# Norm roots as a power on GpSimd and softmax reciprocals between two 32x32 block transposes, in a transformer layer on one core

## The reference

```
x = x + layernorm(attention(layernorm(x)))
x = x + layernorm(ffn(layernorm(x)))

layernorm(x) = (x - mean) / sqrt(var + 1e-5)          # no weights
attention:  c_kv = x W_DKV + b, c_q = x W_DQ + b       # latent width 128
            k_c, v = c_kv W_UK + b, c_kv W_UV + b;  q_c = c_q W_UQ + b
            k_r, q_r = (x W_KR + b) * pe, (x W_QR + b) * pe
            per head (16 of width 32): k = [k_c, k_r], q = [q_c, q_r]
            softmax(q k^T / sqrt(32)) v, then W_O + b
ffn:        shared relu(x up)^2 down, plus 2 of 16 experts chosen per token
```

## Time and profile before

| | us |
|---|---|
| median of 3 runs | 1858.47 (1858.25 to 1858.62) |
| the profiled execution | 1858.86 |
| its span, first to last instruction | 1857.0 |
| attention units, all 32 | about 62 to 1085 of the span |

### The profile page before, as it was taken

The page is one execution under the profiler, slowest core; times in us unless marked ns, Lnnn a source line. Parts: engine busy times, 40 slices in busy tenths (PEclk is TensorE's granted clock), DMA queues, the critical chain, the costliest instruction groups (busy, mean ns, idle before and its releaser), DMA issues.

```text
span 1857.0 us, 21713 instructions
## 1 busy us (share of the span) xinstructions
PE 1703.8 (92%) x7194; PEld 1042.3 (56%) x7194; DVE 1030.8 (56%) x2133; ACT 828.4 (45%) x1465; POOL 726.6 (39%) x627
## 2 busy tenths in 40 slices
PE   5898989989989989989899788999999999988998
PEld 2444535435445445444444346888766666656886
DVE  2666577567676685684755635444511111116998
ACT  2345355355355454454454434443133333336554
POOL 0355465456455455563655642000122222214341
PEclk9798999989989999999989889999799999999999
DMA  5654455356355364462554332412473333448773
GB/s 157 174 155 123 121 143 181 84 152 181 86 165 152 93 187 123 136 190 77 150 162 150 100 114 79 164 46 97 132 264 131 126 127 132 127 141 299 240 240 123
DMA packets 123365, 270.51 MB, mean 146 GB/s; under 512 B 14996, under 2 KB 26644, under 8 KB 117108
## 3 DMA queue, kind: packets, MB, share of 16 engines
q1 hardware_dynamic: 96856, 205.93, 36.7%
q0 software_dynamic: 12912, 41.82, 7.1%
q10 hardware_dynamic: 13488, 21.37, 3.1%
HBM read 153.99 MB, written 92.01 MB: 132 GB/s over the span
## 4 chain that ended last, share of the span: by engine, by line
PE 66%; DVE 22%; DMA 4%; ACT 3%; issue 3%; POOL 1%; SPq 1%; DVEq 0%; ACTq 0%; POOLq 0%
PE bank L616 9%; PE bank L594 8%; PE bank L672 7%; PE bank L695 7%; DVE a L804 6%; PE bank L553 6%; PE bank L536 5%; PE bank L476 5%; DVE a L810 3%; PE bank L521 3%; PE bank L507 3%; PE bank L525 3%; PE bank L492 2%; PE bank L545 2%; DVE a L735 2%
## 5 line engine op out<-in xcount | busy, mean ns | idle before, releaser
L1449 POOL TENSOR_TENSOR a<-a 128x512 f32<-128x512 f32 x384 | 483.0, 1284 | 475.2 <-ACT a L1261 475.2
L1261 ACT ACTIVATE a<-bank 128x512 f32<-128x512 f32 x512 | 299.8, 595 | 258.2 <-PE bank L525 252.0
L804 DVE TENSOR_REDUCE a<-bank 128x1 f32<-128x512 f32 x512 | 325.2, 668 | 96.4 <-PE bank L507 95.9
L521 PE MATMUL bank<-a 128*128 128x512 f32 x512 | 281.6, 550 | 50.1 <-ACT a L1261 50.0
L507 PE MATMUL bank<-a 128*128 128x512 f32 x512 | 203.0, 434 | 28.5 <-DVE a L804 20.1
L525 PE MATMUL bank<-a 68*128 68x512 f32 x512 | 209.4, 409 | 0.3 <-ACT a L1251 0.2
L594 PE MATMUL bank<-c 128*128 128x512 f32 x768 | 186.8, 401 | 22.8 <-ACT c L1306 8.4
L521 PEld LDWEIGHTS bank<-a 128*128 128x128 f32 x512 | 100.1, 196 | 180.1 <-ACT a L1261 98.8
L1116 DVE TENSOR_TENSOR f<-f 128x256 f32<-128x256 f32 x79 | 33.6, 425 | 268.2 <-ACT f L1378 268.2
L594 PEld LDWEIGHTS bank<-c 128*128 128x128 f32 x768 | 146.2, 192 | 62.3 <-issue 13.2
L616 PE MATMUL bank<-c 128*128 128x512 f32 x768 | 176.8, 390 | 3.4 <-DVE c L854 1.7
(11 more groups left out here) (176 smaller groups left out, 2093.7 us busy)
## 6 DMA issues: line engine op xcount, KB each, us to landing
a<-kq_scratch SPq DMA_DIRECT2D x192, 256.0 KB, 5.6
kq_scratch<-a SPq DMA_DIRECT2D x32, 1024.0 KB, 4.1
a<-a SPq DMA_DIRECT2D x80, 256.0 KB, 5.0
yp_scratch<-f ACTq DMA_DIRECT2D x79, 256.0 KB, 2.0
a<-in_L_attn_x SPq DMA_DIRECT2D x15, 1024.0 KB, 8.5
x_scratch<-a SPq DMA_DIRECT2D x8, 1024.0 KB, 5.1
h_scratch<-a SPq DMA_DIRECT2D x8, 1024.0 KB, 4.3
hT_scratch<-a SPq DMA_DIRECT2D x8, 1024.0 KB, 6.5
```

Of the source, the lines that this page charges most:

```text
L521: e.matmul(SC[n % 2][:], K.Kc[:, z, j, i * P:(i + 1) * P], K.Qc[:, z, j, :], start=True, stop=False)
L804: e.tensor_reduce(K.mx[:, i, j:j + 1], K.MX[n % 3][:], AX.X, ALU.max).then_inc(Z.max, 1)
L1261: e.activation(K.pt[:, n % NP, :], K.SC[n % 2][:], ACT.Exp, scale=SCALE).then_inc(Z.exp, 1)
L1449: e.tensor_tensor(K.acc[:, j, :], a, K.pt[:, n % NP, :], ALU.add).then_inc(Z.acc, 1)
```

## The change

The change does four things.

- The norm's root leaves VectorE, with L742 and L759. GpSimd does it in eight instructions on 128x4 numbers: add epsilon, a power with exponent -0.5 (a tensor_tensor against a tile of -0.5), one Newton step in four, and offset and scale. Each but the last waits for the one before. It starts when the variances of the four tiles are there (semaphore var).
- A norm's labels are still seven: the three of the root are now pause, root, pause.
- ScalarE's copy of the denominators (L1274) is gone. VectorE reads them from PSUM with a block transpose (every 32x32 block for itself), takes the reciprocal of one column in 32, a 128x16 tile, and writes them back to 128x512 with a second block transpose that reads each number 32 times. The bank of "total" is given back by the reciprocal, so by VectorE's place in its order and no longer by ScalarE's.
- The labels of it are four in place of five: total, invert, pause, divide. GpSimd's multiplication is "divide", where it stood with the fourth reciprocal.

```diff
 def norm_order(kind, b):
-    return ([("stat", kind, b, 0), ("stat", kind, b, 1)] + [("root", kind, b, s) for s in range(3)]
-            + [("scale", kind, b, 0), ("scale", kind, b, 1)])
+    return [("stat", kind, b, 0), ("stat", kind, b, 1), ("pause",), ("root", kind, b), ("pause",), ("scale", kind, b, 0), ("scale", kind, b, 1)]
 def normalise_order(u):
-    return [("total", u)] + [("invert", u, n) for n in range(4)]
+    return [("total", u), ("invert", u), ("pause",), ("divide", u)]
 def vector_program
-    def invert(u, n):
-        cut = slice(n * P, (n + 1) * P)
+    def invert(u):
+        bank = begin("total", u)
+        if u:
+            w.wait_ge(Z.cx, u)
+        e.transpose(K.rden, bank[:]).then_inc(Z.dT, 1)
+        w.wait_ge(Z.dT, u + 1)
+        e.reciprocal(K.dr, K.rden[:, 0:S:HD]).then_inc(*end("total", u))
         m = K.fill["total", u]
         w.wait_ge(Z.free[m % 2], m // 2 + 1)
-        e.reciprocal(K.rden[:, cut], K.rden[:, cut]).then_inc(Z.rden, 1)
+        e.transpose(K.rden, K.dr.unsqueeze(2).broadcast_to([P, S // HD, HD])).then_inc(Z.rden, 1)
 def scalar_program
-    def total(u):
-        bank = begin("total", u)
-        if u:
-            w.wait_ge(Z.cx, u)
-        e.copy(K.rden, bank[:]).then_inc(*end("total", u))
 def gpsimd_program
-    def invert(u, n):
+    def divide(u):
         g = u % NG
-        if n == 3:
-            w.wait_ge(Z.kept, u + 1)
-            w.wait_ge(Z.rden, 4 * (u + 1))
-            e.tensor_tensor(K.ctxT[:, g, :], K.ctxT[:, g, :], K.rden, ALU.mult).then_inc(Z.cx, 1)
+        w.wait_ge(Z.kept, u + 1)
+        w.wait_ge(Z.rden, u + 1)
+        e.tensor_tensor(K.ctxT[:, g, :], K.ctxT[:, g, :], K.rden, ALU.mult).then_inc(Z.cx, 1)
+    def root(kind, b):
+        mv, nw = K.mv[kind], K.nw[kind]
+        ve, t, r = nw[:, 0, :], nw[:, 1, :], nw[:, 2, :]
+        w.wait_ge(Z.var[kind], 4 * (b + 1))
+        if b:
+            w.wait_ge(Z.scaled[kind], 4 * b)
+        e.tensor_scalar(ve, mv[:, :, 1], EPS, None, ALU.add).then_inc(*chain.next())
+        w.wait_ge(Z.root, chain.n)
+        w.wait_ge(Z.half, 1)
+        e.tensor_tensor(r, ve, K.mhalf, ALU.pow).then_inc(*chain.next())
+        w.wait_ge(Z.root, chain.n)
+        e.tensor_tensor(t, r, r, ALU.mult).then_inc(*chain.next())
...
+        e.tensor_tensor(r, r, t, ALU.mult).then_inc(*chain.next())
+        w.wait_ge(Z.root, chain.n)
+        e.tensor_tensor(nw[:, 3, :], mv[:, :, 0], r, ALU.mult).then_inc(Z.off[kind], 1)
+        e.tensor_scalar(nw[:, 4, :], r, -1.0, None, ALU.mult).then_inc(Z.off[kind], 1)
```

More of the change, by code:

```diff
@@ L288, in __init__ @@
         self.ones, self.small, self.sel, self.rope = make("ones_set"), make("dve_step"), make("sel_set"), make("rope_done")
+        self.var = {k: make(f"var_{k}") for k in KINDS}
         self.off = {k: make(f"off_{k}") for k in KINDS}
+        self.half, self.root = make("half_set"), make("root_step")
+        self.dT, self.dr = make("dT_done"), make("dr_done")
         self.scaled = {k: make(f"scaled_{k}") for k in KINDS}
@@ L342, in attention_room @@
     K.ones = tile([P, HD])
+    K.mhalf = tile([P, 4])
+    K.dr = tile([P, S // HD])
     K.stats = {"n": tile([P, 4, 6])}
@@ L721, in stat @@
     def stat(kind, b, half):
-        stats, mv, nw = K.stats[kind], K.mv[kind], K.nw[kind]
+        stats, mv = K.stats[kind], K.mv[kind]
         src = {"n": K.xt, "y": K.yb, "h": K.xb}[kind]
@@ L736, in stat @@
             at[i] = small.n
+        if b and not half:
+            w.wait_ge(Z.off[kind], 2 * b)
         for i in (2 * half, 2 * half + 1):
             w.wait_ge(Z.small, at[i])
[L739 to L759, removed]
+            e.bn_aggr(mv[:, i, :], stats[:, i, :]).then_inc(Z.var[kind], 1)
     def sel():
@@ L1173, in finish @@
         e.tensor_tensor(K.x1[:, z, :], K.x1[:, z, :], K.sh[:, z, :], ALU.add).then_inc(Z.co, 1)
-    stages = {"stat": stat, "root": root, "sel": sel, "proj": proj, "half": half, "bias": bias, "top": top, "invert": invert,
+    stages = {"stat": stat, "sel": sel, "proj": proj, "half": half, "bias": bias, "top": top, "invert": invert,
               "project": project, "route": route, "split h": split_h, "split up": split_up, "split down": split_down, "up": up,
@@ L1207, in scale @@
         src, out = {"n": (K.xt, K.xt), "y": (K.yb, K.yb), "h": (K.xb, K.yb)}[kind]
-        w.wait_ge(Z.off[kind], b + 1)
+        w.wait_ge(Z.off[kind], 2 * (b + 1))
         for i in (2 * half, 2 * half + 1):
@@ L1417, in scalar_program @@
     stages = {"scale": scale, "turn": turn, "proj": proj, "v": v, "half": half, "rows": rows, "scores": scores, "keep": keep,
-              "total": total, "turn2": turn2, "split h": split_h, "split up": split_up, "round up": round_up,
+              "turn2": turn2, "split h": split_h, "split up": split_up, "round up": round_up,
               "round down": round_down, "up": up, "store": store, "choose early": choose, "e turn": e_turn, "e up": e_up,
@@ L1436, in gpsimd_program @@
     e.memset(K.ones[:], 1.0).then_inc(Z.ones, 1)
+    e.memset(K.mhalf, -0.5).then_inc(Z.half, 1)
+    chain = Steps(Z.root)
     def scores(u, i, j):
@@ L1449, in scores @@
         e.tensor_tensor(K.acc[:, j, :], a, K.pt[:, n % NP, :], ALU.add).then_inc(Z.acc, 1)
-    def invert(u, n):
+    def divide(u):
         g = u % NG
-        if n == 3:
-            w.wait_ge(Z.kept, u + 1)
-            w.wait_ge(Z.rden, 4 * (u + 1))
-            e.tensor_tensor(K.ctxT[:, g, :], K.ctxT[:, g, :], K.rden, ALU.mult).then_inc(Z.cx, 1)
+        w.wait_ge(Z.kept, u + 1)
[14 more added lines that the diff above has]
+        w.wait_ge(Z.root, chain.n)
+        e.tensor_tensor(t, t, ve, ALU.mult).then_inc(*chain.next())
+        w.wait_ge(Z.root, chain.n)
+        e.tensor_scalar(t, t, 0.5, -1.5, ALU.mult, ALU.add).then_inc(*chain.next())
+        w.wait_ge(Z.root, chain.n)
+        e.tensor_tensor(r, r, t, ALU.mult).then_inc(*chain.next())
+        w.wait_ge(Z.root, chain.n)
+        e.tensor_tensor(nw[:, 3, :], mv[:, :, 0], r, ALU.mult).then_inc(Z.off[kind], 1)
+        e.tensor_scalar(nw[:, 4, :], r, -1.0, None, ALU.mult).then_inc(Z.off[kind], 1)
     def scale(kind, b, half):
@@ L1513, in gather @@
         e.indirect_dma_start(K.yc[:, z, :], None, K.yp_d, bass.IndirectOffsetOnAxis(K.sl2[:, t:t + 1], 0)).then_inc(Z.cg[z], 16)
-    stages = {"scores": scores, "invert": invert, "scale": scale, "split down": split_down, "choose early": choose,
+    stages = {"scores": scores, "divide": divide, "root": root, "scale": scale, "split down": split_down, "choose early": choose,
               "store": store, "fetch": fetch, "gather": gather}
@@ L1731, in program @@
     K.fill = {x: n for n, x in enumerate(x for x in K.order if x[0] in FILLS)}
-    K.at_root = {}
     with ExitStack() as ctx:
```

## The result

| | before | changed |
|---|---|---|
| median us, 5 runs each | 1858.25 (1857.02 to 1858.62) | 1875.33 (1868.7 to 1876.06) |
| ratio | 1 | 1.0085, 95% interval 1.0067 to 1.0102 |
| span of the profiled execution | 1857.0 | 1873.4 |
| TensorE's mean granted clock | 0.946 | 0.948 |

What follows compares the result with a forecast made beforehand. TensorE's waits were taken as the bound, chiefly 50.0 us for exponentials, plus lower clock behind them. Waits -33, clock -35, bank against maxima 0, last reciprocals -2 made -70 us from 1858.86: 1790, 8-in-10 range 1758 to 1862.

Steps and rivals of the forecast that it cites:

- bank against maxima: Before half q: TensorE's new wait for total's bank, about 50 us, offset by fewer waits for maxima; 0, ends -20 and +30.
- The clock: Behind the y and h scalings: shorter waits avoid the lower granted clock, 35 us back, 21 at h and 14 at y.
- The waits at the scalings: TensorE's waits for exponentials at seven y and seven h norms: 7.5 to 2.8 us a pair, 33 us saved.
- R: Length of a norm's root on GpSimd: 2.4 us taken, lower bound 1.6, upper 6.7.
- R - 1.4: TensorE's wait left at a norm h scaling: 1.0 us in place of 3.6.
- R - 0.6: TensorE's wait left at a norm y scaling: 1.8 us, where ScalarE stood 3.93 before.
- The last term: End of the kernel: the last unit's four reciprocals, which nothing hides, -2 us.
- GpSimd's queue behind the root: Three sums behind the root on GpSimd: late by half a microsecond, covered unless the root takes over about 4 us.
- rival (a): The root's power on GpSimd is slow, so scaling waits grow: about 1895 us; chance 0.18, three quarters of it slower.
- Rival (b): Before half q: slow transposes or unrecovered bank waits eat the gain, +30 to +45, 1820 to 1835 us; chance 0.14.
- Rival (c): In shorter units the stack through DRAM or GpSimd's load becomes a new bound: 1825 us; chance 0.13.
- the signs that it named for being wrong: Power over 2 us, clock still 0.55 behind waits of 1 to 2 us, or g = 0 units over 1 us longer.

Runs made afterwards that it cites:

- root_only: The kernel before with the norm part of the change alone (root on GpSimd, reciprocals as before): 1842.87 us, ratio 0.9928.
- recip_only: The kernel before with the reciprocal part of the change alone (two transposes and a 128x16 reciprocal, roots on VectorE): 1875.41 us, ratio 1.01.
- recip_early_only: The kernel before with the reciprocal part alone, VectorE's transposes and reciprocal issued at the label total: 1812.87 us, ratio 0.977.
- invert_early: The changed kernel with VectorE's two transposes and reciprocal issued at the label total, ahead of half k: 1806.32 us, ratio 0.9724.
- root_early: The changed kernel with the root two labels earlier, ahead of both pauses: 1855.7 us, ratio 0.9995.
- power_twice: The changed kernel with the power issued a second time in each root, same result: 1904.14 us, ratio 1.0255.

## Why the prediction was wrong, by its own steps

**The failing step is the pair "bank against maxima", put at 0.** Its first half was right nearly to the digit: 1.6 us a unit were forecast, 1.51 measured in three units of a batch, 2.12 in g = 0 where 2.2 was forecast, 48.3 us over 29 units against "about 50". The second half, what VectorE gives back, was taken from one g = 0 unit followed, which came out even, and carried to all. That unit is the one where it is wrong: it got 2.3 us longer, with 1.0 us more of waits (2.1 in place of 1.1) and 1.7 us more of clock loss. What came back in all is 20.1 - 1.8 = 18.3 us before plain scores, against 48.3. (The 11.9 us that went before the transposes of the maxima belong to the norm part: root_only has them at 4.8, recip_only at 14.2.) So in waits alone the pair is +30, the very end of its range of -20 to +30, and that range had no clock in it. In the six g = 0 units of the middle the clock cost 1.1 us before and 10.4 now. The first three and the last four units, not looked at, lost 9 and 8 us. recip_only and recip_early_only price the place of the three instructions at 62.5 us, invert_early at 69.

**The clock was counted for one wait and not for the other.** The forecast gave 35 us back for shorter waits at the scalings, and charged nothing for a new one of 1.5 us in 30 units, on the strength of a 0.90 us wait with a full-speed matmul behind it. Measured, the clock loss stayed at 97 against 100 us. Windows of the kernel before and of the changed one show how it moved: g = 0 units go from 1.00 to 0.96, g = 2 from 0.90 to 0.97.

```profile
309.00:345.00 36.00, 34.92 (x144) 18.20 (x144) 17.15 (x26) 14.09 (x26) 16.22 (x13) 1.00 0.32 88
...
381.00:411.20 30.20, 25.85 (x108) 12.70 (x104) 23.04 (x42) 16.68 (x29) 17.46 (x15) 0.90 0.62 191
```

```profile
317.00:356.00 39.00, 36.89 (x156) 19.26 (x148) 16.47 (x26) 14.18 (x25) 16.32 (x13) 0.96 0.31 81
...
392.00:421.00 29.00, 25.07 (x108) 12.21 (x106) 15.78 (x29) 16.21 (x29) 21.69 (x24) 0.97 0.64 186
```

The last four units fell from 0.94 to 0.87 (972 to 1085 and 982.5 to 1104 us). What the forecast wanted back at the scalings came in part: in the twelve units with g = 1 and g = 2 of batches 0 to 5 the clock loss fell from 31.8 to 12.2 us, 20 where 30 was forecast, for behind ten of the twelve shorter waits, 1.9 to 2.4 us, the clock still fell, for about half as long. And the bank's waits took it away again. Not all of them did: behind the 17 waits of 1.5 us ahead of half q, all in units with g = 1, 2 and 3, the clock stayed at 1.00, so the 0.90 us wait had not misled there; behind each of the nine of 2.1 us it fell. One of each, the window behind the wait at 427.1 (g = 3) and behind the one at 456.4 (g = 0):

```profile
427.10:436.00 8.90, 8.90 (x45) 5.87 (x46) 8.81 (x18) 5.68 (x10) 6.50 (x6) 1.00 0.59 184
456.40:462.00 5.60, 5.60 (x20) 3.46 (x20) 4.09 (x7) 2.48 (x4) 2.85 (x3) 0.70 0.37 152
```

The length of a wait alone does not decide it: in root_early the clock fell behind only four of the same nine waits of 2.1 us. Either repair alone brought some 21 us of clock back. That a clock term exists and is of this size was right; that only the scalings have it was wrong.

**The waits at the scalings: -33 forecast, -8.8 measured over all of the waits for exponentials.** In batches 0 to 5 the twelve waits went from 43.7 to 27.0 us. R was 2.94, not 2.4: the power's 0.85 us on top of a small instruction was as forecast (0.8), the small ones were 0.28 us apart and not 0.23. For h, R - 1.4 would be 1.5; measured 2.0. For y, R - 0.6 would be 2.3; measured 2.39, but by two errors that cancel: "proj r" moved a label ahead, so exponentials 12 and 13 both come behind it and the root starts a sum later after it than the step had it, while TensorE gets to its wait later too. In batch 6, in the last units, the waits grew, from 0.81 and 1.52 to 3.21, 1.72 and 1.52 us; the forecast had taken all fourteen as alike. One in the third unit grew from 1.69 to 3.63. And not all of the gain is the root's: recip_only, with the root on VectorE, has 3.08 us at y in place of 3.94.

**The last term, -2 us for the reciprocals of the last unit,** can't be told: what comes behind the last keep took 773.6 us before and 771.3 in the changed kernel, and 765.5 to 772.8 in the others.

**Right as put:** that the root is worth taking off VectorE (root_only gains 14 us; that VectorE's small instructions get longer beside GpSimd's sums is in the trace, but no run tells how much of the gain that is); the transposes, 0.69 forecast against 0.71; the reciprocal, 0.25 against 0.25; GpSimd's queue behind the root covered; rival (a), the slow power, is out, and power_twice, at 26 us for each further microsecond, suggests that it would have cost more than it said (its own terms, 14 x 2.1 and 14 x 1 us, make 1902 and not 1895). Rival (b) had the right mechanism and too small a price, since it took the gain as given and added 30 to 45 to it; the waits alone are its 30. Rival (c) comes up once the bank is repaired: 22.0 us for the stack, and with the early root 16.4 for the sums. Its load of GpSimd was misread: the four additions of x belong to norm y, in the unit with g = 1, and a g = 2 unit had 14 instructions of 1.28 us before, not 17. Of the signs that it named for being wrong, the one on g = 0 units came (2.3 us longer, against 1), the one on the power did not (1.04 us), and the one on the clock came in part.

## What to carry to other kernels

When an evacuation moves from one engine's queue to another's, ask who writes that bank next and what stands ahead of the new reader in its own order: here one maximum and one projection, whose own input had to go round two engines, turned 44 us of gain into 19 of loss (recip_early_only and recip_only). Price every wait that a change adds with the same second term that you give to those it removes. A stretch followed is worth something only for its own kind of unit; the first and the last ones were the dear ones. When a stretch gets shorter, look at what its DMAs come closer to.

The version to keep is the changed kernel with VectorE's part of the reciprocals at "total": 1806.3, or 1803.5 with the root two labels earlier, which the runs do not tell apart.

## What the runs showed of the hardware

- A power on GpSimd against a 128x4 tile takes 1.04 us (24 times, 1.036 to 1.33), five times a multiplication of that size (0.20). None of them shows the 6 us that the prediction had named as an estimate for freshly loaded code. Once, ahead of the first root, such a time could be hidden: GpSimd stands idle there for 6.04 us, until VectorE's statistics end.
- A 32x32 block transpose of 128x512 fp32 took 0.706 us from PSUM and 0.711 from SBUF, the second with each number read 32 times.
- In the changed kernel the granted clock fell behind none of 17 TensorE waits of 1.5 us and behind all nine of 2.1 us; in root_early behind four of nine of 2.1 us.
- Of copies of 1024 KB to DRAM, one issued 5.9 us behind a load of 1024 KB landed 4.4 us later, one issued 1.6 us behind such a load 9.6 us later, and four between them fall in order (the table in the experiments).
